# Ending a turn of a woven top-384 sort at the join: merge and flip move into the next turn, and so do down products

## The chip, the cores and the metric

One core of one Trainium2 chip runs the whole program. The metric is device time in microseconds (us) from launch to end; the kernel before takes 7146.54 us (median of 3 runs, 7143.46 to 7152.91). The core has TensorE (PE, matmuls into PSUM), VectorE (DVE), ScalarE (ACT) and GpSimd (POOL) for elementwise work, and SyncE (SP), which here issues the weight loads. Each engine works through its own queue in order; semaphores tie the queues together.

## The reference, cut to what matters

A graph network over 625 nodes of 768 features is followed by a mixture layer. The change lies in the mixture layer alone:

```python
pe = softmax(posembed @ pos_w + pos_b)                  # 16 experts x 768
y = (silu(h @ sg_w) * (h @ su_w)) @ sd_w                # shared perceptron, 1536 wide
for i in range(16):
    feature = h * pe[i] @ gate_w + gate_b               # 625 x 768
    weight, idx = top_k(feature, 384)                   # sorted, the upper half
    weight = softmax(weight)
    u = take_along_axis(h, idx, -1) * weight            # 625 x 384
    y = y + (silu(u @ eg_w[i]) * (u @ eu_w[i])) @ ed_w[i]
yn = layernorm(y) * ln_g + ln_b
return x + silu(yn @ m1_w + m1_b) @ m2_w + m2_b
```

All values are float32. The top_k is a full sort network on 768 keys per token with the value of `h` carried along as payload.

## The kernel before, in words

**Layout.** The 625 tokens are 5 tiles of 125 tokens on the partitions; a partition holds 5 x 768 keys (`key`) and as many payloads (`pay`). The 768 features are three runs of 256 (`BLK`, `RUN`), interleaved, so that one instruction sorts all three.

**Stages and units.** `STAGES` has 55 stages: 36 of an ordinary bitonic sort of the three runs, the **join** of the first two runs into `key_top`, 8 **merge** stages on it, the **flip**, which compares the lower part of the merged run with the third run backwards, and 9 **bitonic** stages that order the best 384. A stage is one or two **units** (`UNITS`), each of at most 960 to 1024 comparisons per partition. There are 93 units for one expert: 56 of the first 28 stages, in halves (`HALVES`), 27 from stage 28 to the flip (`WHOLES`), and 10 behind the flip (`TOPS`).

**A unit.** ACT copies one side of the comparison into a PSUM bank (`seed`); DVE writes the larger keys (`larger_keys`, L1479) and the smaller ones (`smaller_keys`, L1489); PE subtracts the larger keys from the seed, which leaves a mask that is not zero where the sides changed places (`mask_ps`, L1154); ACT and POOL save the first payloads or their sum with the second (L1398, L1241); DVE moves payloads under the mask (`first_pays`, L1511, and `second_pays`, L1528); POOL gets its share of the second payloads as sum minus first (L1249). POOL takes 4/8 of the second payloads in a streamed unit and 3/8 in another (`shares`).

**Turns and order.** The order on every engine is written out by hand. `OPENING` is expert 0's `HALVES + WHOLES`. `REGULAR` is `WOVEN + WHOLES`: the ten `TOPS` of expert i-1 alternate with the first ten `HALVES` of expert i; then the other halves run alone, then the wholes. `CLOSING` is the `TOPS` of expert 15. Where `u < turn.streams`, a unit depends only on units up to u-2 (`Turn.needs`), and DVE puts other units' work between its own steps. In the wholes a unit depends on the whole stage before it. PE, ACT and POOL run the same list with their own parts. The DVE, ACT, PE and POOL queues loop over turns 1 to 14 (`Fori`); turn 15 and the closing are written out after it.

**Products beside the sort.** `beside` spreads TensorE products over the units of a turn in proportion to the comparisons; each product's parts are issued behind the mask of their unit, with ACT one unit later and POOL two. `beside_all` has two stretches: `ahead` for the units before `BEGIN` and the rest up to three units before the end of the turn. In a loop turn the first holds the gate products of expert i+1 (four token tiles); the second holds expert i-1's perceptron: transposes (`turn_tile`), gate and up products (`mixed`), the fifth tile's gate products, and down products (`down`). The shared perceptron is four **pieces**: two beside the opening, two beside turn 15, in which nothing stands in the first stretch. `PAUSE` is a gap in the list as wide as a product. The perceptron of expert 15 runs alone after the closing.

**Loads.** `w_exp` holds an expert's gate and up weights and then its down weights, or a piece's; each load waits for a count of filled PSUM slots (`filled`), so it cannot start before the products on the old contents are done.

## Time and profile before

| | |
|---|---|
| runs | 7143.46, 7146.54, 7152.91 us |
| profiled execution, its own time | 7141.31 us |
| its span | 7139.5 us |
| mean granted TensorE clock | 0.942 |
| busy: PE / DVE / POOL / ACT | 6041.2 / 5404.9 / 3578.1 / 2689.2 us |
| graph network and preparation | up to 1281.5 us |
| opening | 1281.5 to 1601.3 us |
| turn 1 | 1601.3 to 1945.0 us |
| turns 2 to 14 | 1945.0 to 6409.6 us |
| turn 15 | 6409.6 to 6865.6 us |
| closing, then the last perceptron | 6865.6 to 6919.2, to 7024 us |
| output stage | 7024 to 7139.5 us |

A turn's border is the start of the L1479 instruction that first reads the next expert's `feat`. Busy time of PE is a union of pipelined records and is no measure of free room by itself. Idle time in brackets behind a row is that of the engine just before the row, with what ended it.

### The profile page before, as it was taken

The numbers are of one execution on the slowest core, as the hardware profiler recorded it, in microseconds if no ns is written. First come the engines' busy times: TensorE is split into PE (matmuls) and PEld (weight loads), VectorE is DVE, ScalarE is ACT, GpSimd is POOL, SyncE is SP. The second block draws the span as 40 slices with busy tenths as digits, with TensorE's granted clock in tenths as the row PEclk, the third lists the DMA queues.
The fourth block names the chain that finished last, engine by engine and source line by source line (L and its number), as shares of the span: only waits on it lengthen the run. The fifth ranks groups of instructions, "written<-read, shape, count | busy, mean of one in ns | idle before, by whom it ended". The sixth has DMA issues, their size and how long they took to land. (4 is left out here: it accounts for less than half of the span.)

```text
span 7139.5 us, 74719 instructions
## 1 busy us (share of the span) xinstructions
PE 6041.2 (85%) x16985; PEld 3123.8 (44%) x16985; DVE 5404.9 (76%) x6633; ACT 2689.2 (38%) x4249; POOL 3578.1 (50%) x3692
## 2 busy tenths in 40 slices
PE   7989988988888878888878888888888888887978
PEld 5545544544443434343434343434343434443534
DVE  3011012789999999999999999999999999998640
ACT  0000000344454545454545444444444444444331
POOL 2333024456564646464656565555556565645430
PEclk9999999999999999999999999999999999998979
DMA  3355256000000000000000000000000000000101
GB/s 89 107 152 161 101 137 165 1 34 1 27 1 27 1 28 13 15 14 14 14 14 14 14 14 14 14 14 14 14 14 14 14 14 27 1 27 27 40 14 48
DMA packets 118188, 262.62 MB, mean 37 GB/s; under 512 B 39164, under 2 KB 49922, under 8 KB 117682
## 3 DMA queue, kind: packets, MB, share of 16 engines
q1 hardware_dynamic: 70322, 180.18, 7.1%
q0 software_dynamic: 47360, 77.17, 4.9%
q14 instruction: 368, 3.01, 0.1%
q8 instruction: 138, 2.26, 0.1%
HBM read 222.43 MB, written 34.58 MB: 36 GB/s over the span
## 5 line engine op out<-in xcount | busy, mean ns | idle before, releaser
L1154 PE MATMUL mask_ps<-key,neg_ident 125*125 125x480 f32 (+7 forms) x4128 | 1925.8, 587 | 583.5 <-DVE key L1489 570.5
L1249 POOL TENSOR_TENSOR pay<-pay_side,pay 125x240 int32<-125x240 int32 (+6 forms) x1104 | 1043.6, 945 | 1291.9 <-DVE pay L1511 1290.4
L1385 ACT COPY mask_ps<-key 125x960 f32<-125x960 f32 (+7 forms) x1136 | 952.4, 838 | 1533.4 <-DVE pay L1528 1031.5
L1154 PEld LDWEIGHTS mask_ps<-key,neg_ident 125*125 125x125 f32 x4128 | 743.9, 196 | 1535.8 <-DVE key L1489 1044.2
L1511 DVE COPY_PREDICATED pay<-mask_ps,pay 125x480 f32<-125x480 int32 (+5 forms) x1104 | 1232.8, 1117 | 195.1 <-PE mask_ps L1154 164.5
L1241 POOL TENSOR_TENSOR pay_side<-pay 125x240 int32<-125x240 int32 (+6 forms) x1104 | 1039.5, 942 | 422.2 <-DVE pay L1528 279.2
L1479 DVE TENSOR_TENSOR key<-mask_ps,key 125x480 f32<-125x480 f32 (+5 forms) x1104 | 1086.2, 984 | 37.8 <-PE mask_ps L1154 37.0
L1489 DVE TENSOR_TENSOR key<-mask_ps,key 125x480 f32<-125x480 f32 (+5 forms) x1104 | 1090.2, 988 | 8.3
L1154 PE MATMUL mask_ps<-key_top,neg_ident 125*125 125x480 f32 (+3 forms) x1472 | 654.8, 574 | 293.8 <-DVE key_top L1489 223.7
L1398 ACT COPY pay_side<-pay 125x480 f32<-125x480 f32 (+6 forms) x1104 | 612.3, 555 | 437.8 <-POOL pay L1249 237.9
L1528 DVE COPY_PREDICATED pay<-mask_ps,pay_side 125x480 f32<-125x480 int32 (+6 forms) x1104 | 742.1, 672 | 41.1 <-DVE pay L1511 31.8
L1100 PE MATMUL slot_ps<-gate_w,xs 128*125 128x384 f32 x1920 | 730.6, 520 | 0.0
L1111 PE MATMUL slot_ps<-w_exp,hid 128*125 128x384 f32 x1920 | 684.3, 495 | 14.3 <-issue 14.3
L1087 PE MATMUL slot_ps<-u_feat,w_exp 128*128 128x312 f32 (+1 forms) x2304 | 663.6, 427 | 0.4 <-ACT u_feat L1316 0.4
L650 PE MATMUL ps_msg<-w_rel,h_feat 128*125 128x384 f32 x1920 | 619.7, 486 | 2.3 <-ACT h_feat L582 2.3
L1249 POOL TENSOR_TENSOR pay_top<-pay_side,pay_top 125x480 int32<-125x480 int32 (+2 forms) x288 | 296.5, 1030 | 544.2 <-DVE pay_top L1511 543.7
L751 POOL DMA_INDIRECT rows_a<-messages_dram,idx_now_a x200 | 242.2, 1211 | 648.2 <-DVE idx_now_a L788 604.1
L1154 PEld LDWEIGHTS mask_ps<-key_top,neg_ident 125*125 125x125 f32 x1472 | 278.5, 209 | 658.6 <-DVE key_top L1489 400.5
L1087 PEld LDWEIGHTS slot_ps<-u_feat,w_exp 128*128 128x128 f32 x2304 | 437.5, 190 | 230.6 <-issue 89.9
L1100 PEld LDWEIGHTS slot_ps<-gate_w,xs 128*125 128x125 f32 x1920 | 365.2, 197 | 354.0 <-issue 186.9
L1111 PEld LDWEIGHTS slot_ps<-w_exp,hid 128*125 128x125 f32 x1920 | 369.4, 193 | 308.0 <-issue 125.2
L661 DVE COPY y_out<-ps_msg 125x768 f32<-125x768 f32 x40 | 38.3, 957 | 611.1 <-PE ps_msg L650 611.1
(179 smaller groups left out, 5914.0 us busy)
## 6 DMA issues: line engine op xcount, KB each, us to landing
w_rel<-L_gnn_W SPq DMA_DIRECT2D x16, 2304.0 KB, 23.4
w_exp<-L_ffn_ed_w SPq DMA_DIRECT2D x16, 2304.0 KB, 8.4
messages_dram<-y_out SPq DMA_DIRECT2D x16, 1875.0 KB
w_exp<-L_ffn_eg_w SPq DMA_DIRECT2D x16, 1152.0 KB, 5.6
w_exp<-L_ffn_eu_w SPq DMA_DIRECT2D x16, 1152.0 KB, 8.1
root_w<-L_gnn_root SPq DMA_DIRECT2D x2, 2304.0 KB
w_exp<-L_ffn_sg_w SPq DMA_DIRECT2D x4, 1152.0 KB, 5.9
w_exp<-L_ffn_su_w SPq DMA_DIRECT2D x4, 1152.0 KB, 8.8
```

Of the source, the lines that this page charges most:

```text
L650: last = pe.matmul(slots[n % 2][0:TP, half, 0:HALF], h_feat[:, k, t * TP:(t + 1) * TP], w_rel[j][:, k, cols], start=(k == 0), stop=(k == K ...
L1087: last = pe.matmul(slots[bank][:, 0:count], weight(bank, k), ins[:, k, first:first + count], start=(k == 0), stop=(k == nk - 1))
L1100: last = pe.matmul(slot, xs[:, t % 2, k, :], gate_w[:, k, cols], start=False, stop=(k == KD - 1))
L1111: last = pe.matmul(slots[bank][0:TP, 0:HALF], hid[:, f, t * TP:(t + 1) * TP], down_w[:, f, half * HALF:(half + 1) * HALF], start=(f == 0), ...
L1154: last = pe.matmul(mask, neg_ident[0:TP, 0:TP], operand, start=False, stop=True, skip_group_check=True)
L1241: pool.tensor_tensor(shares(pay_was(turn, u), turn, u)[1].bitcast(I32), first, second, ALU.add).then_inc(pays_added, 1)
L1249: pool.tensor_tensor(second, shares(pay_was(turn, u), turn, u)[1].bitcast(I32), first, ALU.subtract).then_inc(pays_taken, 1)
L1385: act.copy(seed_of(turn, u), compared(turn, u)[0]).then_inc(seeded, 1)
L1479: dve.tensor_tensor(results(turn, u)[0], seed_of(turn, u), compared(turn, u)[1], ALU.max).then_inc(maxed, 1)
L1489: dve.tensor_tensor(smaller, seed, second, ALU.min).then_inc(minned, 1)
L1511: dve.copy_predicated(larger, mask_of(turn, u), second).then_inc(moved, 1)
L1528: dve.copy_predicated(smaller, mask, was).then_inc(pays_done, 1)
```

## The change

1. `WHOLES` ends at the join. The 8 merge units and 2 flip units of an expert are now the first ten `TOPS`: there are 20, woven with 20 of the next expert's halves. A regular turn still has 93 units (76 woven or halves, 17 wholes); the opening has 73 in place of 83, the closing 20 in place of 10. The unit numbers `EXPS`, `WEIGH`, `INVERT`, `SCALE` and `BEGIN` follow: `BEGIN` is 54 in place of 34.
2. The third run has to outlive the start of the next expert's sort. At the two join units ACT copies its keys (`keep_keys`, 1280 elements) and payloads (`keep_pays`, 2 x 640) into `mlp_in` and a new `third_rest`. The next expert's payload presets (3 copies a turn) stand behind these copies, two before the turn's end.
3. Down products of expert i-2 go into the first stretch of turn i, ahead of the gate products; the second stretch keeps transposes, gate and up products and the fifth tile's gates.
4. Pieces of the shared perceptron: 0 in the opening, 1 in turn 1 (now written out before the loop, which runs 2 to 14), 2 in turn 15, 3 half in the closing and half behind it. Turn 15 also takes expert 13's down products and all of expert 14.
5. `y_part` shares memory with `u_feat`; one wait is added for that (`turned`). Loads wait for the new counts.

```diff
-WHOLES = [unit for unit in UNITS if APART <= unit[0] <= FLIP]
-TOPS = [unit for unit in UNITS if unit[0] > FLIP]
+WHOLES = [unit for unit in UNITS if APART <= unit[0] <= JOIN]
+TOPS = [unit for unit in UNITS if unit[0] > JOIN]
...
@@ sync @@
             load_piece(0, None, None)
...
+            load_piece(1, OPEN_BASE + 2 * SGU, SECOND_BASE)
+            load_expert(0, SECOND_BASE + NEARLY + 2 * SGU, SECOND_IN + NIN)
+            with sync.Fori(1, NEXP - 2) as e:
+                base = LOOP_BASE + (e - 1) * PER_TURN + NHALF
+                load_expert(e, base, base + (NEARLY + NIN))
             sync.wait_ge(feat_ready, NEXP * NHALF)
...
+            load_piece(2, LAST_BASE + NHALF, LAST_BASE + NHALF)
+            load_expert(NEXP - 2, LAST_BASE + NHALF + 2 * SGU, LAST_IN + NIN)
+            load_piece(3, CLOSE_BASE, CLOSE_BASE)
+            load_expert(NEXP - 1, CLOSE_BASE + 2 * SGU, END_BASE + NIN)
...
@@ tensor @@
-            sort(OPENING, 0, beside(OPENING, products, 0, 1, OPENING.n - 3))
-            with pe.Fori(1, NEXP - 1) as i:
-                base = (i - 1) * PER_TURN + LOOP_BASE
-                sort(REGULAR, i, beside_all(REGULAR, gate_products(i + 1, base, range(AHEAD)),
-                                            mlp(i - 1, base + 2 * AHEAD, i + 1), 0))
...
+            sort(OPENING, 0, beside(OPENING, gate_products(1, PIECES) + piece(0, OPEN_BASE), 0, 1, OPENING.n - 6))
+            sort(REGULAR, 1, beside_all(
+                REGULAR, gate_products(2, SECOND_BASE, range(AHEAD)) + piece(1, SECOND_BASE + NEARLY),
+                expert_in(0, SECOND_IN) + gate_products(2, SECOND_IN + NIN, range(AHEAD, NT)), 0))
+            with pe.Fori(2, NEXP - 1) as i:
+                base = LOOP_BASE + (i - 2) * PER_TURN
+                sort(REGULAR, i, beside_all(
+                    REGULAR, expert_out(i - 2, base) + gate_products(i + 1, base + NHALF, range(AHEAD)),
+                    expert_in(i - 1, base + (NHALF + NEARLY))
+                    + gate_products(i + 1, base + (NHALF + NEARLY + NIN), range(AHEAD, NT)), 0))
+            sort(REGULAR, NEXP - 1, beside_all(
+                REGULAR, expert_out(NEXP - 3, LAST_BASE) + piece(2, LAST_BASE + NHALF),
+                expert_in(NEXP - 2, LAST_IN) + [PAUSE] + expert_out(NEXP - 2, LAST_IN + NIN), 0))
+            sort(CLOSING, NEXP, beside(CLOSING, piece_in(3, CLOSE_BASE), 0, 1, CLOSING.n - 3))
+            now(piece_out(3, CLOSE_BASE))
+            now(expert_in(NEXP - 1, END_BASE))
+            now(expert_out(NEXP - 1, END_BASE + NIN))
...
@@ scalar, sort @@
+                    if turn.units[u] == (JOIN, 0, 2):
+                        keep_keys()
+                    if turn.units[u] == (JOIN, 1, 2):
+                        keep_pays()
+                    if turn.units[u] == (JOIN, 1, 2) and following is REGULAR:
+                        act.wait_ge(kept, i * NKEPT + NKEPT)
+                        preset(0)
+                        act.wait_ge(pays_done, turn.done("units", i, u))
+                        preset(1)
                     do(todo.get(u, []))
-                    if following is REGULAR and JOIN + 2 <= turn.units[u][0] < JOIN + 2 + NSET - 1:
-                        preset(turn.units[u][0] - (JOIN + 2))
...
@@ scalar, end @@
             for t in range(NT):
                 exponentials(NEXP - 1, t)
+            now(piece_out(3, CLOSE_BASE))
             act.wait_ge(inv_ready, NEXP)
```

How the instructions move on three engines (key tile, payload tile or PSUM tile in front of the arrow, what is read behind it):

VectorE, merge units of expert 14 with distances 16 and 8. Before, in the wholes:

```order
L1479 TENSOR_TENSOR key_top<-mask_ps,key_top 125x12x80
L1489 TENSOR_TENSOR key_top<-mask_ps,key_top 125x12x80
L1511 COPY_PREDICATED pay_top<-mask_ps,pay_top 125x6x160
L1528 COPY_PREDICATED pay_top<-mask_ps,pay_side 125x3x160
L1479 TENSOR_TENSOR key_top<-mask_ps,key_top 125x24x40
L1489 TENSOR_TENSOR key_top<-mask_ps,key_top 125x24x40
```

Now, in the next turn, woven with halves of the next expert:

```order
L1557 TENSOR_TENSOR key<-mask_ps,key 125x32x30
L1580 COPY_PREDICATED pay_top<-mask_ps,pay_top 125x6x160
L1547 TENSOR_TENSOR key_top<-mask_ps,key_top 125x12x80
L1597 COPY_PREDICATED pay_top<-mask_ps,pay_side 125x3x160
L1557 TENSOR_TENSOR key_top<-mask_ps,key_top 125x12x80
L1580 COPY_PREDICATED pay<-mask_ps,pay 125x32x30
L1547 TENSOR_TENSOR key<-mask_ps,key 125x32x15
```

The four steps of a merge unit no longer stand in a row, each behind the one it reads; steps of `key` and `pay` stand between them. The number of steps is the same.

ScalarE, the end of a turn, from the last whole or join seeds to the first seed of the next turn's unit 1. Before (end of the opening):

```order
L1385 COPY mask_ps<-key_top 125x2x320
L1385 COPY mask_ps<-feat 125x64x15
L1452 UNCONDITIONAL_BRANCH
L1452 ISA
L1382 ISA
L1384 REGISTER_ALU
L1385 COPY mask_ps<-key_top 125x640
```

Now (end of turn 1):

```order
L1451 COPY pay_top<-pay 125x640
L1452 COPY pay_top<-pay 125x640
L1417 COPY mlp_in<-key 125x1280
L1441 COPY mask_ps<-feat 125x64x15
L1451 COPY pay_top<-pay 125x640
L1452 COPY pay_top<-pay 125x320
L1422 COPY mlp_in<-pay 125x640
L1422 COPY third_rest<-pay 125x640
L1430 COPY pay<-h_tok 125x256x5
L1430 COPY pay<-h_tok 125x128x10
L1515 UNCONDITIONAL_BRANCH
```

Between the seed from `feat` and the first seed of the next turn from `key_top` there now stand six copies.

TensorE, turn 15, where piece 2 begins. Before, behind expert 14's down products in the middle of the halves:

```order
L1111 MATMUL slot_ps<-w_exp,hid 125x384 x3
L1087 MATMUL slot_ps<-h_feat,w_exp 128x313 x3
L1154 MATMUL mask_ps<-key,neg_ident 125x4x120
L1154 MATMUL mask_ps<-key,neg_ident 125x3x120
L1087 MATMUL slot_ps<-h_feat,w_exp 128x313 x9
```

Now, behind expert 13's down products among the woven units:

```order
L1183 MATMUL mask_ps<-key,neg_ident 125x8x45 x2
L1130 MATMUL slot_ps<-w_exp,hid 125x384 x3
L1183 MATMUL mask_ps<-key_top,neg_ident 125x512
L1183 MATMUL mask_ps<-key_top,neg_ident 125x128
L1106 MATMUL slot_ps<-h_feat,w_exp 128x313 x3
```

The piece still stands directly behind products that use the same weight tile, with one unit's mask between them, and there are one or two products to a mask where there were two to four.

## Rows read from the trace of the kernel before

**Rows 1.** The page: busy time of the engines, and granted clock in 40 slices.
```profile
PE 6041.2 (85%) x16985; PEld 3123.8 (44%) x16985; DVE 5404.9 (76%) x6633; ACT 2689.2 (38%) x4249; POOL 3578.1 (50%) x3692
...
PEclk9999999999999999999999999999999999998979
```

**Rows 2.** Busy time in stretches; first line has the columns.
```profile
core 0: us, PE busy (x) PEld busy (x) DVE busy (x) ACT busy (x) POOL busy (x), PEclk, DMA share, GB/s
1281.50:1601.30 319.80, 291.77 (x856) 160.49 (x857) 289.33 (x327) 141.22 (x222) 180.69 (x191) 0.97 0.05 18
1558.60:1601.30 42.70, 36.56 (x102) 18.47 (x102) 36.98 (x37) 20.52 (x30) 26.01 (x26) 0.97 0.13 50
1601.30:1790.60 189.30, 159.61 (x421) 77.80 (x420) 177.77 (x218) 93.31 (x154) 118.01 (x121) 0.93 0.01 2
1756.00:1790.60 34.60, 32.15 (x101) 17.96 (x100) 34.60 (x42) 17.00 (x31) 24.16 (x25) 1.00 0.00 1
1756.00:1891.40 135.40, 118.65 (x338) 60.96 (x337) 131.04 (x146) 60.03 (x96) 78.45 (x86) 0.99 0.05 18
1903.80:1945.00 41.20, 31.62 (x83) 15.54 (x84) 37.04 (x38) 18.20 (x25) 21.02 (x20) 0.94 0.16 58
1945.00:6409.60 4464.60, 3745.91 (x9998) 1834.63 (x9997) 4194.02 (x4811) 2095.68 (x3302) 2577.71 (x2691) 0.95 0.04 15
6409.60:6865.60 456.00, 374.04 (x1041) 205.31 (x1039) 325.25 (x371) 169.42 (x286) 219.67 (x233) 0.89 0.09 32
6865.60:6919.20 53.60, 28.77 (x40) 10.79 (x40) 38.16 (x42) 13.21 (x19) 18.46 (x20) 0.56 0.00 0
```

**Rows 3.** What VectorE waited for in one loop turn (us, times, longest).
```profile
DVE pay L1511 <- PE mask_ps L1154: 7.6, 5, 3.2
```

**Rows 4.** VectorE in order of time, a merge unit in the wholes (start, us).
```profile
1916.66 1.14 DVE L1479 TENSOR_TENSOR key_top<-mask_ps,key_top 125x960 f32<-125x960 f32 x1
...
1920.30 0.70 DVE L1528 COPY_PREDICATED pay_top<-mask_ps,pay_side 125x480 f32<-125x480 int32 x1 [0.15 <-DVE pay_top L1511]
1921.04 1.16 DVE L1479 TENSOR_TENSOR key_top<-mask_ps,key_top 125x960 f32<-125x960 f32 x1
```

**Rows 5.** VectorE in order of time, a woven unit of the same size.
```profile
2310.85 1.15 DVE L1479 TENSOR_TENSOR key<-mask_ps,key 125x960 f32<-125x960 f32 x1
...
2314.70 1.15 DVE L1479 TENSOR_TENSOR key_top<-mask_ps,key_top 125x960 f32<-125x960 f32 x1
```

**Rows 6.** TensorE and VectorE among the woven units of turn 1.
```profile
1648.83 4.20 PE L1100 MATMUL slot_ps<-gate_w,xs 128*125 128x384 f32 x6
...
1655.17 1.23 DVE L1511 COPY_PREDICATED pay<-mask_ps,pay 125x960 f32<-125x960 int32 x1 [3.11 <-PE mask_ps L1154]
...
1656.61 1.77 PE L1154 MATMUL mask_ps<-key_top,neg_ident 125*125 125x480 f32 x4
```

**Rows 7.** ScalarE at a join unit and a preset; VectorE behind the loop's edge.
```profile
1901.05 0.80 ACT L1396 COPY pay_top<-pay 125x640 f32<-125x640 f32 x1
...
1948.18 1.41 ACT L1374 COPY pay<-h_tok 125x1280 f32<-125x1280 f32 x1 [0.84 <-DVE pay_top L1505]
...
1950.39 0.82 DVE L1479 TENSOR_TENSOR key_top<-mask_ps,key_top 125x640 f32<-125x640 f32 x1 [2.25 <-issue]
```

**Rows 8.** VectorE in turn 15, where piece 2's weights are waited for.
```profile
6665.20 1.09 DVE L1511 COPY_PREDICATED pay<-mask_ps,pay 125x840 f32<-125x840 int32 x1 [13.04 <-PE mask_ps L1154]
```

**Rows 9.** Closing: VectorE starts one unit, TensorE makes its mask, VectorE starts the next.
```profile
6904.02 1.16 DVE L1479 TENSOR_TENSOR key_top<-mask_ps,key_top 125x960 f32<-125x960 f32 x1 [1.75 <-PE mask_ps L1154]
...
6906.42 3.55 PE L1154 MATMUL mask_ps<-key_top,neg_ident 125*125 125x480 f32 x4 [2.52 <-DVE key_top L1489]
...
6910.09 0.66 DVE L1479 TENSOR_TENSOR key_top<-mask_ps,key_top 125x480 f32<-125x480 f32 x1 [1.74 <-PE mask_ps L1154]
```

**Rows 10.** TensorE behind the closing: expert 15's perceptron.
```profile
6926.50 1.51 PE L1075 MATMUL slot_ps<-ident,mlp_in 125*128 125x125 f32 x6 [9.59 <-ACT mlp_in L1411]
...
6931.90 40.71 PE L1087 MATMUL slot_ps<-u_feat,w_exp 128*128 128x313 f32 x144 [0.35 <-ACT u_feat L1316]
...
6981.31 40.73 PE L1111 MATMUL slot_ps<-w_exp,hid 128*125 128x384 f32 x120 [8.70 <-issue]
```

More of the change, by code:

```diff
@@ L912, in compared @@
         def compared(turn, u):
-            s = turn.units[u][0]
-            return [part_in_banks(side, turn, u) for side in pair((feat if s == 0 else key)[:, :], key_top[:, :], STAGES[s])]
+            s, part, parts = turn.units[u]
+            first, second = pair((feat if s == 0 else key)[:, :], key_top[:, :], STAGES[s])
+            if s == FLIP:
+                second = third_key[:, ::-1, :]
+            return [part_in_banks(side, turn, u) for side in (first, second)]
         def results(turn, u):
@@ L922, in results @@
                 return part_in_banks(larger, turn, u), fewer(smaller, turn, u)
-            larger, smaller = [part_in_banks(side, turn, u) for side in pair(key[:, :], key_top[:, :], STAGES[s])]
-            return larger, None if s == FLIP else smaller
+            larger, smaller = pair(key[:, :], key_top[:, :], STAGES[s])
+            return part_in_banks(larger, turn, u), None if s == FLIP else part_in_banks(smaller, turn, u)
         def payloads(turn, u):
-            s = turn.units[u][0]
-            first, second = [part_in_banks(side, turn, u) for side in pair(pay[:, :], pay_top[:, :], STAGES[s])]
+            s, part, parts = turn.units[u]
+            first, second = pair(pay[:, :], pay_top[:, :], STAGES[s])
+            first = part_in_banks(first, turn, u)
+            second = in_banks(third_pays[1 - part][:, ::-1, :]) if s == FLIP else part_in_banks(second, turn, u)
             if s != JOIN:
@@ L1135, in mlp, with downs @@
-            def mlp(e, base, gate_of=None):
+                return [(mixed, (base + n, side, ins, nk, weight(f), first, count, inputs if n == 0 else None,
+                                 loads if n == 0 else None), parts)
+                        for n, ((f, first, count, side), parts) in enumerate(zip(places, mixed_parts(nk, nf)))]
+            def downs(base, nf, down_w, loads, hids):
+                return [(down, (base + n, n % 2, t, half, nf, down_w, loads, hids if n == 0 else None), parts)
+                        for n, (t, half, parts) in enumerate(halves_of(down_parts(nf)))]
@@ L1147, in sort, with now @@
+            def piece(q, base):
+                return piece_in(q, base) + [PAUSE] + piece_out(q, base)
+            def now(products):
+                for work, args, parts in products:
+                    for part in range(len(parts)):
+                        work(*args, part)
             def sort(turn, i, todo):
@@ L1308, in _, with turned @@
                 weigh(NEXP - 1, t)
-            for work, args, _ in mlp(NEXP - 1, END_BASE):
-                work(*args)
+            now(downs(CLOSE_BASE + 2 * SGU, KK))
+            now(expert_in(END_BASE))
+            now(expert_out(END_BASE + NIN))
         @block.scalar
         def _(act):
-            def turned(n, bank, t, first, last):
+            def turned(n, bank, ys, t, first, last):
+                if t == 0:
+                    act.wait_ge(y_added, ys + 1)
                 act.wait_ge(filled, n + 1)
@@ new lines, in downs, with expert_in @@
+            def downs(base, nf, ys):
+                return [(summed, (base + n, n % 2, ys, t, half), parts)
+                        for n, (t, half, parts) in enumerate(halves_of(down_parts(nf)))]
+            def expert_in(e, base):
+                turns = [(turned, (base + n, n % 2, before(e, NHALF, NHALF), *place), parts)
+                         for n, (place, parts) in enumerate(zip(TURNS, turn_parts))]
+                return turns + hiddens(base + NTURN, KK, KD, before(e, NGU, SGU))
@@ new lines, in expert_out, with piece_in, piece_out, now @@
+            def expert_out(e, base):
+                return downs(base, KD, before(e, NHALF, NHALF))
+            def piece_in(q, base):
+                return hiddens(base, KD, KK, before_piece(q, NGU, SGU))
+            def piece_out(q, base):
+                return downs(base + 2 * SGU, KK, before_piece(q, NHALF, NHALF))
+            def piece(q, base):
+                return piece_in(q, base) + [PAUSE] + piece_out(q, base)
+            def now(products):
+                for work, args, _ in products:
+                    work(*args)
```

214 lines of the change are left out of this document (101 added, 113 removed).

## The prediction

> **What bounds the kernel now.** I read the page's first line, then stretches between turn borders, then VectorE's waits, then single units. By the page PE is the busiest engine, 6041 us against DVE's 5405 [rows 1]. The stretches say otherwise: in the 13 loop turns from 1945.0 to 6409.6, 343.4 us each, DVE is busy 322.6 us and PE 288.1 [rows 2]. In such a turn DVE waits for PE masks 7.6 us [rows 3]. So VectorE is the bound in the loop, by 94%, and what a turn costs is its number of DVE steps, the price of a step, and a few waits. Turn 15 is another regime: 456 us, DVE busy only 325 [rows 2]; beside it stand expert 14's perceptron and two pieces, all behind unit 34. The closing is a third: 53.6 us for 10 units, PE busy 28.8, clock 0.56 [rows 2], each unit a chain.
>
> The Trainium skill (Perfetto Trace Analysis, Identifying the Most-Contended Engine) says that matmul busy time is a poor measure of how near PE is to its limit, since records are pipelined. The trace agrees, since weight loads are busy only 44% of the span beside PE's 85% [rows 1]. If PE's busy time were real work, turn 15 after the change would hold about 338 us of it (288 and the 50 us of products below) where I find 327.
>
> **1. Merge and flip woven.** A merge unit of 960 in the wholes takes 4.38 us from L1479 to the next L1479; its last step starts behind a 0.15 us wait for its third [rows 4]. A woven unit of 960 takes 3.85 [rows 5], because DVE fills each such wait with another unit's step. The ten units now cost 41.2 us a turn [rows 2]. Woven: 7 x 3.85, about 2.7 for the merge unit of 640, and 3.0 for the two flip units, which have two steps instead of four (both scaled from the 960 unit): 32.7. Gain 8.5 a turn. Lower bound zero, if POOL's larger share (4/8 for 3/8) sets the pace; upper bound 10, if the flip units, with half the steps, come at half my price for them.
>
> **2. The border of a turn.** ScalarE gets a queue there: join copies (0.80 each), the keys (1280 elements), two halves of the payloads, two presets; a copy of 1280 took 1.41, one of 640 took 0.80 [rows 7]. The seed from `feat` comes after the first join's two copies and the keys: 0.8 + 0.8 + 1.4 + 1.0 = 4.0 us behind the last whole's payloads, when DVE has some 3.7 us of other steps (0.82 for each of 640 [rows 7]): 0.3 wait. Then 1.3 (join), 1.6 (payloads), 2.8 (presets), so the next key_top seed ends some 10.3 us behind the same point, and DVE is ready at about 7.6: 2.7 us, plus up to 1.8 if ScalarE's own loop edge comes on top. Today the border has a 2.25 us wait of DVE at the loop edge [rows 7], which would lie inside the new one. I take 1 us worse a turn. Bounds: 3 better, 6 worse (all 6 us of copies exposed). Queued behind these copies is only the new turn's seeds, and DVE waits for those.
>
> **3. Products in the first stretch.** 20 down parts and 16 gate parts over 53 units, in place of 16 over 33; the second stretch has 34 in 36 in place of 54 in 56. A mask of 960 costs PE 1.77 at the high level [rows 6], a down part (three matmuls) 40.73/20 = 2.04, a gate or up part 40.71/24 = 1.70 [rows 10], a gate half some 4.7. First stretch: 42,240 comparisons make 78 us, downs 41, gates 38: 157 of 187 us. Second: 57 + 4 + 41 + 9 = 111 of 135. So there is room and no cost by load. What the clock does is the open part: where a unit has no product, PE stands still, and then six records take 4.20 us, twice their 2.1, and DVE waits 3.11 [rows 6]; clock 0.93 in units 0 to 53 of turn 1 but 1.00 in units 44 to 53, where products are dense [rows 2]. Fewer empty units in the first stretch, but it is longer: I put zero, bounds 5 us either way.
>
> Turn net: 8.5 - 1 = 7.5, thirteen times: **-97.5**.
>
> **4. Opening.** Ten units go, 42.7 us [rows 2]. Its PE load falls from 294 us (masks 125, gates 47, two pieces at 41 + 20) of 319.8 to about 215 of 272: I take 8 us of the waits with it (bounds 0 and 13), and add 3 for the new border: **-47.7**.
>
> **5. Turn 1** gets a piece (61 us of PE) in place of the downs (41) in the first stretch: 178 of 187, 95% full. I take 6 us against the 7.5: **-1.5**.
>
> **6. Turn 15.** DVE's floor is 343.4 - 7.5, less 2.2 as it has no loop edge: 333.7. First stretch: masks 78, downs 41, piece 61: 180 of PE; DVE's own time there is 189.3 - 34.6 + 32.7 = 187.4 [rows 2]. Second: masks 57, transposes 4, 41 + 41: 143 of PE against DVE's 135.4 [rows 2]. The opening ran at 294/320 = 92% of such load; at 94% these make 192 and 152: 5 and 16 above DVE. The piece's weights cannot be asked for before expert 13's last down product, and one mask lies between: today's such wait is 13.04 us [rows 8]; with one unit's cover 10. The expert's own down weights have a pause and three masks, some 12 us, for a load. 333.7 + 5 + 16 + 10 = 364.7 for 456.0: **-91.3** (bounds -120, nothing but DVE's floor, and -55, loads exposed twice and 88% of PE).
>
> **7. Closing.** The ten units come here, unwoven: 42.7 as in the opening. But PE now has 24 parts of piece 3 beside it. Today a closing unit of 960 takes 6.07 us from L1479 to L1479, because the mask needs 3.55 us and DVE waits 1.74 for it [rows 9]; with the mask at 1.77 it would be the 4.38 of [rows 4], with 0.2 for products in the way. Five tops at -1.5, eight merges at +0.2: 42.7 + 1.6 - 7.5: **+36.8**. If the clock stays low there: 25 more. The Trainium skill (TensorE: Matmul & The Clock Gate, What's actually happening) has the throttled state as the default and sustained activity as what releases it. By that rule one and a half products a unit should lift the closing's clock; the trace agrees as far as 0.56 in the bare closing and 0.97 in the opening go [rows 2].
>
> **8. Behind the closing.** Ten down halves of piece 3 (20.4 us of PE) now stand on PE and ScalarE ahead of expert 15's transposes. Today there are 9.6 us of idle PE there [rows 10]. Two halves fit in before ScalarE, busy with exponentials, empties a slot; the other eight follow at 2.04. First transpose some 26.5 us behind the last mask, not 9.6: **+17** (bounds 11, only the excess over the idle time, and 24, with the first at the low clock). The exposed load before the last downs, 8.70 [rows 10], stays.
>
> **Sum.** -97.5 - 47.7 - 1.5 - 91.3 + 36.8 + 17 = -184.2. On the span of 7139.5 that is 6955.3; the profiled execution's own time was 1.8 above its span, and the median of the runs 5.2 above that: **6962 us**.
>
> **The rivals.**
> - *The border becomes the wait.* All copies exposed and the loop edge behind them: 5 us more a turn, 14 times, 70: about 7030. For it: ScalarE is in strict order, and the second seed stands behind six copies. Against: a copy costs 0.8 to 1.41 [rows 7] and DVE has 7 us of own work.
> - *The clock stays high.* The denser first stretch ends most of the 7.6 us that DVE waits for masks in a turn [rows 3], say 5, in 14 turns: 70 less, 6892. For it: 1.00 where products are dense [rows 2]. Against: a third of the first stretch's units stay empty.
> - *Turn 15 keeps its bound*: PE work there falls only from 374 busy to some 327; loads exposed twice: 40 back, 7002.
> - *Weaving gains nothing*, so the change doesn't do what it says: POOL's two steps of 1.0 each and down additions of 1.0 set a pace of 4.4 for the woven merges. 8.5 x 14 = 119 back: 7081. Against: POOL is busy 58% of a turn [rows 2].
> - *The slower side: the clock falls in the first stretch.* Down parts come one by one with gaps. Each fall that meets a product costs 3.1 us of DVE [rows 6]. 184 us over 14 turns are 13 a turn: from 4.2 more falls a turn on, the change loses; at 5 it is 7180. Against: today 16 parts over 33 units leave five waits and 7.6 us in a whole turn [rows 3], and the new stretch has 36 over 53.
>
> **Numbers.** Forecast 0.60, border 0.13, clock high 0.11, turn 15 0.08, weaving 0.04, slower side 0.04. The forecast's own range, from the bounds of parts 1 to 8 taken together as independent, is 6925 to 7000; with border, turn 15 and half of the clock case the range is 6900 to 7030. What a measurement of this kernel can tell from no change is about 0.2%, 14 us. Faster 0.94, same 0.02, slower 0.04.
>
> **What would show it.** Part 1: from the start of one expert's first `feat` unit to the next, 336 us in the loop; DVE busy about 318 of it; woven merges at 3.85. Part 2: DVE's wait for ACT or at the loop edge before the first unit of `key_top`, 2.5 to 5 us. Part 3: granted clock 0.93 to 0.97 in units 0 to 53. Part 6: turn 15 at 365 us and one wait of about 10 for the piece's weights. Part 7: closing of about 90 us with a clock over 0.9 and units of 4.6. Part 8: first transpose 26 us behind the last mask. The forecast is wrong if the loop turns stay over 341 or fall below 331, or if turn 15 stays over 400.

## The result and the profile after

The kernel after takes 6935.49 us (median of 4 runs, 6922.95 to 6938.25), the kernel before on the same chip 7149.73 us: a ratio of 0.9696, 95% interval 0.9684 to 0.9708. The forecast was 6962 us, range 6900 to 7030, so the time is 26.5 us below the forecast and inside the range. The profiled execution is the fastest of the four (6922.95 us, span 6921.2) and 12.5 us below their median; the sums below are of it.

Page of the kernel after: busy time, and the granted clock in 40 slices.

```profile
PE 5904.7 (85%) x16985; PEld 3098.9 (45%) x16985; DVE 5366.8 (78%) x6633; ACT 2729.2 (39%) x4297; POOL 3589.6 (52%) x3692
...
PEclk9989999999999999999999999999999999999999
```

The shares hardly differ from [rows 1]: PE 85% and DVE 76% then, 85% and 78% now. They say nothing of a gain of 3%; the stretches do. The windows below are opening, turn 1, turns 2 to 14, the two stretches of products in one loop turn (units 0 to 53, 54 to 92), turn 15 and closing (columns as in [rows 2]).

```profile
1287.70:1551.60 263.90, 228.71 (x610) 113.56 (x610) 251.12 (x290) 115.84 (x179) 153.14 (x162) 0.94 0.04 14
1551.60:1891.70 340.10, 296.60 (x854) 158.02 (x853) 320.44 (x370) 168.74 (x271) 203.33 (x213) 0.95 0.04 15
...
1891.70:6237.20 4345.50, 3640.49 (x9998) 1814.91 (x9997) 4162.04 (x4811) 2128.69 (x3342) 2583.55 (x2688) 0.96 0.04 15
...
2223.00:2406.00 183.00, 158.64 (x427) 76.70 (x428) 177.50 (x213) 92.28 (x144) 117.10 (x117) 0.96 0.04 14
2406.00:2558.00 152.00, 122.41 (x344) 63.52 (x342) 142.55 (x159) 71.47 (x115) 82.19 (x91) 0.94 0.04 16
6237.20:6591.40 354.20, 320.20 (x953) 179.34 (x953) 321.78 (x370) 169.59 (x280) 215.57 (x227) 0.95 0.09 32
6591.40:6679.00 87.60, 73.83 (x231) 44.09 (x232) 73.99 (x77) 32.93 (x53) 39.88 (x41) 0.93 0.10 35
```

| part | before | after | change | forecast |
|---|---|---|---|---|
| graph network | 1281.5 | 1287.7 | +6.2 | 0 |
| opening (4) | 319.8 | 263.9 | -55.9 | -47.7 |
| turn 1 (5) | 343.7 | 340.1 | -3.6 | -1.5 |
| turns 2 to 14 (1 to 3) | 4464.6 | 4345.5 | -119.1 | -97.5 |
| turn 15 (6) | 456.0 | 354.2 | -101.8 | -91.3 |
| closing (7) | 53.6 | 89.2 | +35.6 | +36.8 |
| last mask to first transpose (8) | 9.6 | 28.0 | +18.4 | +17.0 |

The closing is taken to VectorE's last step in both kernels, at 6919.2 and 6680.6 us; the window above ends 1.6 us earlier, and so do the 87.6 us of the expectations. The parts of the change sum to -226.4. The graph network gave 6.2 back, and 1.9 lie in the last perceptron and the output. The graph network is the same in all kernels here and ends between 1275.7 and 1295.4 us in their profiled executions, so a few us of a single execution are its spread.

A loop turn, VectorE in order of time: a woven unit of 960, from its first step to the first step of the next unit (`key` to `key_top`), answering [rows 5]; then the border, answering [rows 7].

```profile
2249.58 1.14 DVE L1547 TENSOR_TENSOR key<-mask_ps,key 125x960 f32<-125x960 f32 x1
...
2253.43 1.14 DVE L1547 TENSOR_TENSOR key_top<-mask_ps,key_top 125x960 f32<-125x960 f32 x1
...
2222.92 1.16 DVE L1547 TENSOR_TENSOR key<-mask_ps,feat 125x960 f32<-125x960 f32 x1 [0.39 <-ACT mask_ps L1441]
...
2229.42 0.82 DVE L1547 TENSOR_TENSOR key_top<-mask_ps,key_top 125x640 f32<-125x640 f32 x1 [2.67 <-PE mask_ps L1183]
```

The woven unit takes 3.85 us, the forecast's price. At the border VectorE waits 0.39 and 2.67 us, where the prediction had 0.3 and 2.7. That the second is put down to PE, whose mask was long there, is a hint that something unnamed came last (runs e4 and e7 below).

What had not been forecast: TensorE near the end of a loop turn (turn 4), and VectorE beside it. Below them stand the mask and VectorE's step at the same place in turn 2, then a window of 20 us there and one in turn 4 (the granted clock stands behind POOL's busy time, as in [rows 2]).

```profile
2852.74 1.68 PE L1183 MATMUL mask_ps<-key,neg_ident 125*125 125x480 f32 x4 [0.25 <-DVE key L1557]
2857.10 3.23 PE L1183 MATMUL mask_ps<-key,neg_ident 125*125 125x480 f32 x4 [2.68 <-DVE key L1557]
2860.25 1.20 PE L1117 MATMUL slot_ps<-gate_b,ones 1*125 1x384 f32 x2
...
2865.21 1.16 DVE L1547 TENSOR_TENSOR key<-mask_ps,key 125x960 f32<-125x960 f32 x1 [1.95 <-PE mask_ps L1183]
...
2190.38 1.88 PE L1183 MATMUL mask_ps<-key,neg_ident 125*125 125x480 f32 x4 [2.68 <-DVE key L1557]
...
2196.84 1.16 DVE L1547 TENSOR_TENSOR key<-mask_ps,key 125x960 f32<-125x960 f32 x1 [0.29 <-PE mask_ps L1183]
...
2185.00:2205.00 20.00, 14.14 (x37) 6.08 (x36) 18.80 (x19) 8.39 (x13) 8.54 (x12) 1.00 0.33 118
2852.00:2872.00 20.00, 14.55 (x30) 6.02 (x29) 17.30 (x18) 6.92 (x10) 8.04 (x10) 0.83 0.32 118
```

On the mean of turns 3 to 14 units 86 and 88 cost 7.11 and 4.85 us, in turn 2 4.63 and 4.43, while their neighbours cost 4.2 to 4.5 in all of them; turn 2 takes 331.2 us, the others 333.9 to 335.1.

Turn 15, its piece's weights; the closing, one unit; behind the closing (answering [rows 8], [rows 9] and [rows 10]).

```profile
6326.08 3.50 PE L1106 MATMUL slot_ps<-h_feat,w_exp 128*128 128x313 f32 x6 [7.84 <-DMA w_exp<-L_ffn_su_w]
6332.17 1.14 DVE L1580 COPY_PREDICATED pay<-mask_ps,pay 125x720 f32<-125x720 int32 x1 [10.40 <-PE mask_ps L1183]
...
6625.28 1.16 DVE L1547 TENSOR_TENSOR key_top<-mask_ps,key_top 125x960 f32<-125x960 f32 x1 [0.76 <-PE mask_ps L1183]
...
6629.86 0.82 DVE L1547 TENSOR_TENSOR key_top<-mask_ps,mlp_in 125x640 f32<-125x640 f32 x1
...
6676.33 1.46 PE L1183 MATMUL mask_ps<-key_top,neg_ident 125*125 125x480 f32 x2 [2.56 <-DVE key_top L1557]
6677.59 5.43 PE L1130 MATMUL slot_ps<-w_piece_down,hid 128*125 128x384 f32 x12
6687.41 17.33 PE L1130 MATMUL slot_ps<-w_piece_down,hid 128*125 128x384 f32 x48 [4.39 <-ACT u_feat L1380]
6705.83 1.04 PE L1094 MATMUL slot_ps<-ident,mlp_in 125*128 125x125 f32 x6 [1.08 <-ACT mlp_in L1467]
...
6759.48 40.34 PE L1130 MATMUL slot_ps<-w_exp,hid 128*125 128x384 f32 x120 [8.49 <-issue]
```

The piece's weights cost one wait of 10.4 us (forecast 10), a closing unit 4.58 us (forecast 4.6) for 6.07, and the first transpose begins 28.0 us behind the last mask's end (forecast 26.5).

### The profile page after: what moved, and what is told of

It is laid out like the page before. It is cut to its first block and busy times, and to the rows that moved or that the text cites. A ratio compares the mean times of both kernels' runs of the same rounds, so it can differ in the third digit from the quotient of the medians.

```text
span 6921.2 us, 74102 instructions
## 1 busy us (share of the span) xinstructions
PE 5904.7 (85%) x16985; PEld 3098.9 (45%) x16985; DVE 5366.8 (78%) x6633; ACT 2729.2 (39%) x4297; POOL 3589.6 (52%) x3692
## 5 line engine op out<-in xcount | busy, mean ns | idle before, releaser
L1183 PE MATMUL mask_ps<-key_top,neg_ident 125*125 125x480 f32 (+3 forms) x1472 | 591.9, 528 | 229.2 <-DVE key_top L1557 216.6
L1119 PE MATMUL slot_ps<-gate_w,xs 128*125 128x384 f32 x1920 | 700.3, 502 | 0.0
L1441 ACT COPY mask_ps<-key_top 125x960 f32<-125x960 f32 (+2 forms) x320 | 278.2, 869 | 586.8 <-DVE pay L1597 450.8
L1183 PEld LDWEIGHTS mask_ps<-key_top,neg_ident 125*125 125x125 f32 x1472 | 258.7, 194 | 548.7 <-DVE key_top L1557 369.8
```

The lines of the kernel that those rows point to most:

```text
L1119: last = pe.matmul(slot, xs[:, t % 2, k, :], gate_w[:, k, cols], start=False, stop=(k == KD - 1))
L1183: last = pe.matmul(mask, neg_ident[0:TP, 0:TP], operand, start=False, stop=True, skip_group_check=True)
L1441: act.copy(seed_of(turn, u), compared(turn, u)[0]).then_inc(seeded, 1)
```

## The experiments

Diffs are against the kernel after. "Loop turn" is the mean of turns 2 to 14 in the profiled execution, from one first `feat` unit to the next.

| run | us, median | ratio to before, 95% | loop turn |
|---|---|---|---|
| before / after | 7149.73 / 6935.49 | 0.9696 (0.9684 to 0.9708) | 343.4 / 334.3 |
| e1 | 7196.09 | 1.0075 (1.0059 to 1.009) | 351.3 |
| e2 | 7280.99 | 1.0187 (1.0171 to 1.0203) | 361.9 |
| e3 | 7013.15 | 0.9815 (0.98 to 0.983) | 335.4 |
| e4 | 6929.15 | 0.9702 (0.9689 to 0.9715) | 335.0 |
| e5 | 6876.15 | 0.9613 (0.9598 to 0.9629) | 331.1 |
| e6 | 6925.67 | 0.9682 (0.9666 to 0.9698) | 335.3 |
| e7 | 6912.02 | 0.9667 (0.965 to 0.9684) | 334.3 |
| e8 | 6877.49 | 0.9615 (0.9601 to 0.963) | 331.7 |
| e9 | 6867.96 | 0.9616 (0.9602 to 0.963) | 331.1 |
| e10 | 6864.3 | 0.9607 (0.9594 to 0.9621) | 331.0 |
| e11 | 6854.08 | 0.9576 (0.956 to 0.9592) | 331.0 |
| e12 | 6844.09 | 0.9569 (0.9555 to 0.9582) | 330.5 |

**e1, weaving undone.**

```diff
-WHOLES = [unit for unit in UNITS if APART <= unit[0] <= JOIN]
-TOPS = [unit for unit in UNITS if unit[0] > JOIN]
+WHOLES = [unit for unit in UNITS if APART <= unit[0] <= FLIP]
+TOPS = [unit for unit in UNITS if unit[0] > FLIP]
-        BEGIN = SCALE + NT
+        BEGIN = SCALE + NT + 10
```

> Merge and flip are taken out of the weaving again (they follow the join in their own turn, one by one), all else stays: copies kept by ScalarE, pieces in four turns, down products a turn later, and the two stretches of products part at the same half stage as now. Theory (part 1: weaving saves 8.5 us a turn): ten units cost about 41 us instead of 33.8, so each of the turns 1 to 15 is 7.4 us longer (111 us), the opening gets ten units of 4.2 (306 us for 264), the closing loses them (about 52 for 87.6): in all about +115, 7050 us; loop turns of about 341.5. Rival (the weaving is worth nothing, the loop turns became shorter because the products lie better): at most +30, 6965 us, loop turns of 334 to 336.

Measured: 7196 us, slower than the kernel before. Turns 2 to 14 are 17.0 us longer than after's, turn 1, which has a piece, 25.3 longer; the opening takes 306.0, the closing, which has piece 3 beside half as many units, 70.9 for the forecast 52. The direction is theory's, the size is twice it (+261 for +115). The ten units cost 49.2 us a turn, where [rows 2] have 41.2. Their window in a turn of e1 has a clock of 0.81 (0.94 before), and VectorE waits again as in the bare closing:

```profile
2951.00:3000.60 49.60, 31.46 (x69) 14.59 (x70) 37.66 (x39) 21.44 (x28) 17.97 (x17) 0.81 0.11 43
...
2960.42 3.56 PE L1183 MATMUL mask_ps<-key_top,neg_ident 125*125 125x320 f32 x8 [5.26 <-DVE key_top L1559]
...
2964.09 1.16 DVE L1549 TENSOR_TENSOR key_top<-mask_ps,key_top 125x960 f32<-125x960 f32 x1 [2.19 <-PE mask_ps L1183]
```

The down products that used to stand beside these units are a turn later: the second stretch has 34 parts for 46 units, where the kernel before has 54 for 56, and so the chained units meet the low level. So 49.2 - 33.7 = 15.5 of the 17.0 us are these units.

**e2, down products back.** `expert_out(i - 2, ...)` leaves the first stretch of turn i, and `expert_out(i - 1, ...)` comes behind the late gate products of the second, on PE, ACT and POOL, with the counts of the loads to match:

```diff
-                    REGULAR, expert_out(i - 2, base) + gate_products(i + 1, base + NHALF, range(AHEAD)),
+                    REGULAR, gate_products(i + 1, base, range(AHEAD)),
...
+                    + expert_out(i - 1, base + (NEARLY + NIN + NLATE)), 0))
```

> The down products of each expert go back into the second stretch of their own turn, behind the gate products; weaving and pieces stay. Theory: with merge and flip woven the second stretch has 39 units and about 152 us of VectorE; TensorE would have masks for 61 us and some 91 us of products there, as much as VectorE has, so TensorE sets the pace: 15 to 20 us more a turn in 14 turns, about 7170 us, slower than the kernel before, second stretch (units 54 to 92) about 170 us with a granted clock near 1.00. Rival (the place of the downs is free, as my zero for part 3 had it): within 5 us a turn, at most 7000 us.

Measured: 7281 us, loop turns 361.9, 27.6 longer than after's. The windows are the two stretches of one of its turns.

```profile
2633.10:2831.10 198.00, 146.96 (x305) 62.90 (x305) 177.57 (x213) 86.88 (x132) 108.83 (x109) 0.82 0.00 1
2831.10:2994.90 163.80, 152.48 (x465) 86.10 (x465) 144.43 (x158) 78.00 (x127) 89.94 (x99) 0.97 0.08 29
```

The second stretch grew from 152.0 to 163.8, with PE busy 93% of it, below theory's 170. The larger half of the loss was not foreseen: the first stretch holds 16 parts in 53 units and grew from 183.0 to 198.0; its clock is 0.82 for 0.96, and single units cost 3 us more (26, 46 and 52: 6.6, 6.8 and 6.1 for 3.8, 3.2 and 2.8). With e1 this makes a square: neither edit 343.4, weaving alone 361.9, later downs alone 351.3, both 334.3 (the two in the middle keep ScalarE's copies and the pieces' new places). Each edit alone loses; together they gain 9.1 a turn. It isn't the mere count of units without a product: by the rule of `beside` a turn has 23 of them before, 24 in e1, 38 in e2 and 22 after. In e1 14 of them lie in the second stretch, where the kernel before has 6.

**e3, last piece back in turn 15.** PE's part; ACT and POOL alike.

```diff
-                expert_in(NEXP - 2, LAST_IN) + [PAUSE] + expert_out(NEXP - 2, LAST_IN + NIN), 0))
-            sort(CLOSING, NEXP, beside(CLOSING, piece_in(3, CLOSE_BASE), 0, 1, CLOSING.n - 3))
-            now(piece_out(3, CLOSE_BASE))
+                expert_in(NEXP - 2, LAST_IN) + [PAUSE] + expert_out(NEXP - 2, LAST_IN + NIN) + piece(3, CLOSE_BASE), 0))
+            sort(CLOSING, NEXP, {})
```

> The last piece of the shared perceptron goes back from the closing into turn 15, behind expert 14's down products; the closing has no products beside it and nothing of the piece follows it. Theory (parts 6 to 8): turn 15 becomes bound by TensorE in its second stretch and waits for the piece's weights, 354 to about 425 us; the closing without products falls to the low clock and its units of 960 take 6.07 us: about 109 us for 87.6; the 18 us behind the closing go, first transpose about 10 us behind the last mask. Sum +73 +21 -18, about 7012 us. Rival (the clock doesn't matter in the closing, products are only in the way there): closing 80 to 86 us, sum about +50, 6986 us.

Measured: 7013 us; turn 15 takes 439.7 (+85.5), the closing 103.8 (+16.2, window for window), and the first transpose starts 9.6 us behind the last mask again (-18.4). Theory holds, with two terms off by 12 and 5 us in opposite directions. That the median hits the forecast to 1 us is luck: the three terms sum to +83, and this trace's loop turns, which the edit leaves alone, add 14 more (335.4 for 334.3; unit 86 costs up to 9.6 us in them). The closing's window, a mask in it, and PE behind it:

```profile
6691.70:6795.50 103.80, 59.48 (x84) 22.58 (x84) 73.91 (x77) 28.64 (x40) 35.03 (x35) 0.57 0.00 0
...
6784.29 3.56 PE L1183 MATMUL mask_ps<-key_top,neg_ident 125*125 125x480 f32 x4 [2.52 <-DVE key_top L1554]
...
6804.40 1.51 PE L1094 MATMUL slot_ps<-ident,mlp_in 125*128 125x125 f32 x6 [9.58 <-ACT mlp_in L1465]
```

Taking work off PE made the closing longer, with VectorE busy 73.9 us as before: clock 0.57 for 0.93, 3.56 us for the mask, 6.08 for a unit of 960. That is part 7's claim shown. The rule of the Trainium skill cited there (TensorE: Matmul & The Clock Gate, What's actually happening) agrees with it.

**e4, the seed first.**

```diff
-                        seed(turn, i, u + 1)
+                        if turn is not REGULAR or u > 0:
+                            seed(turn, i, u + 1)
...
+                        seed(following, i + 1, 1)
                         act.wait_ge(kept, i * NKEPT + NKEPT)
```

> At the border of a turn ScalarE puts the seed of the next turn's second unit (the first of key_top) ahead of the two presets of the payloads, not behind them; nothing is left out. Theory (part 2): the 2.7 us that VectorE waits before that unit are time in ScalarE's queue, so nearly all of them go, 2.5 us in each of 15 turns: -35, 6900 us. Rival (the queue only moves: VectorE now waits for the presets before the first payload step of the new turn, because they come 0.7 us later): -5 to +10, 6930 to 6945 us.

Measured: 6929 us, no gain that can be told. In the loop neither theory nor rival holds: the wait neither went nor moved to the presets. The rows are VectorE's second unit at a border inside the loop and at turn 15's, which is straight code; the third is turn 15's border in the kernel after.

```profile
2229.31 0.82 DVE L1549 TENSOR_TENSOR key_top<-mask_ps,key_top 125x640 f32<-125x640 f32 x1 [2.64 <-PE mask_ps L1183]
...
6247.24 0.80 DVE L1549 TENSOR_TENSOR key_top<-mask_ps,key_top 125x640 f32<-125x640 f32 x1
```

```profile
6242.72 0.82 DVE L1547 TENSOR_TENSOR key_top<-mask_ps,key_top 125x640 f32<-125x640 f32 x1 [1.73 <-ACT mask_ps L1441]
```

In straight code 1.73 us of ScalarE's queue went to nothing, though unit 1 behind it gave about half back (2.90 us in the kernel after, 3.85 to 4.33 at the three straight borders); inside the loop 2.64 stayed. So beneath the first cause lay a second, a little longer one (unit 0 takes 6.4 us inside the loop of the kernel after, 5.9 in turn 2, which begins in straight code): the loop's own edge, which [rows 7] show as 2.25 us of issue.

**e7, a hint at the back edges** (on e4).

```diff
-            with dve.Fori(2, NEXP - 1) as i:
+            with nc.Fori(2, NEXP - 1, engines=bass.OrderedEngineSet([dve.engine]), hint_back_edge=True) as i:
```

> The seed put first as in the run before, and each of the four engines' loops over the experts gets a hint that names its back edge at the top of the body, so that the instructions at its head can be fetched in time; no work changes. Theory now held: with the seed first VectorE still shows 2.6 us before the first key_top unit in the loop turns, but not in turns 1, 2 and 15, whose borders are no back edge; so the loop's back edge costs it 2.1 to 2.7 us, hidden before behind ScalarE's queue. With the hint they go: 2.1 to 2.7 us in 12 turns, -25 to -32 against the seed-first kernel, 6900 us. Rival (the 2.6 us are the price of a taken branch and of the registers, which no fetch changes): 6929 us as before.

```profile
2560.47 0.82 DVE L1549 TENSOR_TENSOR key_top<-mask_ps,key_top 125x640 f32<-125x640 f32 x1 [0.41 <-issue]
```

The wait fell from 2.64 to 0.41, so it was the edge. The Trainium skill (Runtime: NRT & Kernel Launch, Instruction fetch mechanics) has a taken branch out of the fetched window force a fetch before execution goes on; the trace agrees as far as 2.2 us go with the hint; that fetching is what they were is not shown otherwise. But the loop turn went only from 335.0 to 334.3: on the mean of turns 3 to 14 unit 1 gave 0.7 us back, unit 58 0.6, and units 31, 86 and 92 0.1 each. The traces have 13 x 0.7 = 9 us of the 25 to 32 expected. The ratios to the kernel before differ by 0.0035, 25 us, with 15 of uncertainty and on two chips, so whether the sum was theory's stays open; in two turns of this trace the clock stayed high in unit 86, and they took 331.0 us.

**e5, late gate weights.**

```diff
-        gate_parts = [[4 * HALF, 3 * HALF]] * NHALF
+        gate_parts = [[4 * HALF, 3 * HALF]] * (2 * AHEAD) + [[KK * TOK_HALVES[0][1]] * 2] * NLATE
```

> Only the weights of the two late gate halves in the table that spreads the products change (939 for 1536 and 1152): in the second stretch the empty units lie at 58, 64, 67, 73 and 81 in place of 61, 65, 72, 83 and 86, and from unit 82 to 89 each has a product. Theory (in units 86 to 88 TensorE falls to its low level behind a unit without product, a mask of 960 takes 3.2 us for 1.7 and VectorE waits 2 to 3.6 us): units 86 and 88 lose their waits, 3 us less in each of 14 turns, 6893 us. Rival (the fall comes wherever a unit is empty, and the wait moves there): within 10 us of 6935.

Measured: 6876 us. Units 86 and 88 cost 4.24 and 4.43 for 7.11 and 4.85 (mean of turns 3 to 14), unit 82 4.6 for 5.4, while unit 75 costs 0.4 more; the loop turn is 331.1: 3.2 x 13 = 41 us, and theory had 3 in each of 14 turns. The ratios to the kernel before differ by 0.0083, 59 us, with 14 us of uncertainty, a little more than the turns explain. The same masks as above, now with a product before each:

```profile
2848.85 1.88 PE L1183 MATMUL mask_ps<-key,neg_ident 125*125 125x480 f32 x4 [1.11 <-DVE key L1557]
2850.56 1.74 PE L1106 MATMUL slot_ps<-u_feat,w_exp 128*128 128x312 f32 x6
2852.94 1.77 PE L1183 MATMUL mask_ps<-key,neg_ident 125*125 125x480 f32 x4 [0.64 <-DVE key L1557]
```

**e6, the last piece's downs behind expert 15's products.**

```diff
-            now(piece_out(3, CLOSE_BASE))
             now(expert_in(NEXP - 1, END_BASE))
-            now(expert_out(NEXP - 1, END_BASE + NIN))
+            now(piece_out(3, CLOSE_BASE + NIN))
+            now(expert_out(NEXP - 1, END_BASE + NIN + NHALF))
```

> The last piece's ten down halves come behind expert 15's gate and up products, not ahead of its transposes (the piece's hidden values lie in the place of feat meanwhile). Theory (part 8): the transposes start 10 us behind the last mask for 28 (-18); the 20 us of down products now stand where TensorE waited 8.5 us for the expert's down weights, so 12 us of them show: -6, 6929 us. Rival (the 28 us were no cost of the downs but ScalarE's and POOL's work after the sort, the exponentials and scalings): the transposes stay at 20 us or later, sum 0 to +12.

```profile
6696.59 1.51 PE L1097 MATMUL slot_ps<-ident,mlp_in 125*128 125x125 f32 x6 [10.03 <-ACT mlp_in L1475]
...
6701.99 40.15 PE L1109 MATMUL slot_ps<-u_feat,w_exp 128*128 128x313 f32 x144 [0.35 <-ACT u_feat L1361]
6741.98 19.51 PE L1133 MATMUL slot_ps<-w_piece_down,feat 128*125 128x384 f32 x60
6761.33 38.86 PE L1133 MATMUL slot_ps<-w_exp,hid 128*125 128x384 f32 x120
```

Measured: 6926 us. The transposes start 10.0 us behind the last mask, not 28.0, so the rival is out, and the wait for the expert's down weights (8.49) is covered. From the last mask to the last down product the trace is 8.4 us shorter (113.6 for 122.0). Part 8's price is shown. The medians can't tell 6 us.

**e8 to e12, combinations.** e8 is e4 to e7 together; e9 is e8 without hints; e10 is e9 with gate and down products in three parts of two matmuls; e11 adds the hints; e12 loads the third piece's weights into `gate_w`.

Expected of e8:

> All four together: seed first, late gate weights, the piece's downs later, hints at the back edges. Theory: the sum, 6 + 42 + 6 + 28 = 82 us less than 6935, 6853 us. Rival (the waits share one slack, TensorE's queue above all, so that one gain uncovers the other's wait): 6890 us or more.

Expected of e9:

> The last combination without the hints: seed first, late gate weights, the piece's downs later. Theory (the hints gain 1.5 us at the border and lose as much again in units 31 and 58, where waits for masks came up; the other edits add up): 6935 - 59 - 6 - 9 = 6861 us. Rival (the edits share one slack): 6870 to 6880 us, as with late gates alone.

Expected of e10:

> The same, and the gate and down products cut into three parts of two matmuls, not two of three, so that of the 52 units of the first stretch 6 are without a product in place of 17, and of the 36 of the second 3 in place of 5. Theory (VectorE's waits for masks come from the low level that TensorE takes behind a unit without product): the granted clock in the loop rises from 0.95 to 0.98, waits for masks of about 3 us a turn in the first stretch go: 20 to 40 us below the other, about 6830 us. Rival (what is left of waits has another cause, ScalarE's and POOL's copies and the semaphores): within 10 us of the other.

Expected of e11:

> The kernel with the products in three parts, with the hints at the loops' back edges as well. Theory (the hints take 1.5 us of VectorE's wait at each of 12 back edges; that the combination with them was no faster came from TensorE's clock falling in units 30 and 31, whose neighbours have fewer empty units here): 15 to 20 us less, about 6848 us. Rival (VectorE earlier at the border only waits later, whatever the products' place): 6860 to 6868 us, with the loop turns at 331.

Expected of e12:

> That kernel again, and the gate and up weights of the third piece are loaded into the place of the gate weights, which are done with before turn 15, not into the place that expert 13's down products still read (the next stage's weights, loaded there until now, come behind the piece's products). Theory (part 6: 10 us of turn 15 are the wait for these weights): the wait at unit 23 goes, 8 to 10 us less in turn 15, 345 us for 354, the sum 8 to 10 us below the other. Rival (TensorE is the bound of turn 15's first stretch, so the wait only moves): less than 3 us.

e8 missed its sum by 24 us, between theory and rival, and e9 by 7; e10's denser products gave 4 us in the median for the 20 to 40 forecast, and the granted clock in the loop is 0.96 as in e9, so its rival held. (By the rule of `beside` 10 units of a turn are without a product there, for 22 in e9; the expectation had 9 for 22.) In e5 and e8 to e11, which differ by 2.2 us at the border and by 12 such units, the mean loop turn is 331.0 to 331.7. In e11 the 2.2 us won at the border come back in unit 30 (4.5 us in turns 3 to 14, for a mean of 3.3 in e10) as a slow mask behind an idle PE, in unit 4 (5.2 for 4.8) and in unit 1 (3.6 for 2.9):

```profile
5295.97 3.47 PE L1187 MATMUL mask_ps<-key_top,neg_ident 125*125 125x480 f32 x4 [2.48 <-DVE key_top L1570]
...
5299.77 1.23 DVE L1593 COPY_PREDICATED pay_top<-mask_ps,pay_top 125x960 f32<-125x960 int32 x1 [1.83 <-PE mask_ps L1187]
```

Why the clock then falls just there stays open; no run separates it. It is no floor either: e12, whose loop is e11's, took 327.8 and 328.8 us in turns 3 and 4, and unit 30 took 2.9 us in them. e11's ratio is 0.0031 below e10's, just more than the two intervals leave open, while its loop turn is the same: by the turns its rival held, by the median (6854) neither did.

e12 against e11, same chip: turn 15 takes 343.3 for 353.6, unit 23 of it 2.9 us for 13.6. The wait for the piece's weights was worth its 10 us; theory held. (The medians differ by 10 us too, which the intervals of the ratios alone couldn't tell.) e12 is the fastest, 6844 us, 0.9569 of the kernel before and some 91 us under the kernel after, on different chips (their ratios differ by 0.0127, which is 91 us as well).

## Why the prediction was right, and where it was not

- **Bound.** Right: loop turn 334.3 with DVE busy 4162/4345.5 = 96% of it. No reading of page shares gives that.
- **Part 1, weaving.** The size was right: the ten units cost 33.7 woven, 32.7 forecast; single units 3.85. But "8.5 a turn" is a difference to neighbours as they are: with the downs gone from beside them (e1) the same units unwoven cost 49.2, and with the downs left where they were (e2) the kernel is 18.5 a turn slower than before.
- **Part 2, border.** The size was right (0.4 + 2.7), the cause half right. I said that today's loop edge "would lie inside the new one"; e4 and e7 show that the edge is as long as the new wait and a little longer than ScalarE's queue, and that therefore taking the queue away gains nothing inside the loop.
- **Part 3, products.** Zero was the term with the wrong working. Units 0 to 53 took 183.0 us, not 187.4: the denser products ended clock falls in the first stretch. Units 54 to 92 took 152.0 where the forecast's turn leaves 148.5: a fall there that I had not looked for, as I counted products per stretch and not which unit has none. e5 prices it at 3.2 us a turn. The net was within my 5 us either way because the two nearly cancel, which is luck. The larger miss is that I called the move free "by load" and had no rival in which it is what makes weaving pay; e2 shows that it is, 27.6 us a turn.
- **Part 4, opening.** 8.2 better. I gave 8 of a possible 13 us of waits and 3 for the border. Without its ten units the opening before leaves 277.1 us and now takes 263.9: 13.2 us went, my upper bound, and the border's wait stands behind the mark at which the opening ends, in turn 1. VectorE is still idle for 12.8 us. The clock is 0.94, lower than the 0.97 before, and yet the stretch is shorter; PE is busy 87% of it, for 91% before.
- **Part 5, turn 1.** -3.6 for -1.5, with that wait in it.
- **Part 6, turn 15.** Both waits as forecast (10.4), but PE's load was mis-sized: I had 5 + 16 us above DVE's floor; the trace has 354.2 - 334.3 = 20 in all, 10.4 of them the weights, and e12 takes 10.3 away. Against the loop turn of the same trace the first stretch is 14.5 us longer (197.5) and the second 4.8 (156.8). So the 94% packing of PE was too pessimistic by some 10 us, all of it in the second stretch. (My own terms give 323 us of PE for this turn, not 327; the trace has PE busy 320.)
- **Parts 7 and 8.** Right in mechanism and size: +35.6 for +36.8 and +18.4 for +17; e3 shows both by taking them away, and e6 the second.
- **Rivals.** "The clock stays high" was partly true (in the first stretch 4 of its 5 us a turn, less 3.5 given back in the second); "the border becomes the wait" and "weaving gains nothing" were not.

The sum missed by 42.2 us in the profiled execution: 21.6 in the loop, 10.5 in turn 15, 8.2 in the opening, 1.9 in three others. The graph network and the output gave back 8.1, so the profiled execution stood 34 below its forecast; it lies 12.5 below its median, and before's 5.2 below its own, which leaves the 26.5 but for rounding. So the 26.5 us flatter the forecast: its terms erred by 42, and the rest is the choice of the execution and the spread of parts that the change doesn't touch.

## What to carry to other kernels

Price an edit of an interleaved schedule with its neighbours as they will be: here two edits each lose 8 to 18 us a turn without the other and gain 9 together, because one moves the work that keeps TensorE's clock up and the other moves the units that need it. Where a table spreads products over units, list the units that get none, and look there first: most cost nothing, but the waits that e5 removed stood behind one of them. Look at single turns too, not only at their mean: the same instructions ran at either level of the clock in different turns. When a wait ends with a releaser that was long done, suspect a second cause under the first, and compare the same place inside a loop and in straight code before working on either.

## What the runs showed of the hardware

- At a back edge of this loop VectorE waits 2.6 us, with a hint at the head of the body 0.4 (e4, e7), though the turn as a whole got only 0.7 us shorter.
- Behind one unit without a product, 2.7 us of idle PE, the next mask takes 3.2 us for 1.7 in most turns, and with a gate half behind it VectorE waits 2 to 3.6 us (e5 removes it). In turn 2 of the kernel after the same idle time left the mask at 1.88 us, and VectorE waited 0.29.
- A sort chain of 20 units got 16 us shorter by 41 us of matmuls beside it: 87.6 us in the kernel after against 103.8, clock 0.93 against 0.57 (e3).
- The mean turn held at 331.0 to 331.1 us in e5, e9, e10 and e11, although in e11 a wait of 2.2 us at its border was gone; single turns of e12 took 327.8 and 328.8.
